# A perceiver block on one core: gates of the last three tiles ahead of tile 3, a semaphore for read banks, other banks for two tiles

## The reference

```
logits = x @ gate_w.T + gate_b                  # 8 per row
logits = where(in the top 2, logits, -inf)
gate   = softmax(logits)
out    = sum over e of gate[e] * (x @ expert_w[e] + expert_b[e])
x      = x + out
```

## Time and profile before

| | us |
|---|---|
| median of 3 runs | 988.33 |
| runs | 987.59 to 992.7 |
| the profiled execution | 989.81 |
| its span, first to last instruction | 988.1 |
| TensorE busy in the span | 920.4 (93%) |
| VectorE busy | 786.7 (80%) |
| ScalarE busy | 704.7 (71%) |
| GpSimd busy | 377.1 (38%) |
| mean granted TensorE clock | 0.977 |

### The profile page before, as it was taken

One profiled execution on the slowest core, in us unless ns is written; L12 is line 12 of the kernel. 1 busy time (PEld: TensorE's weight loads), 2 busy tenths in 40 slices (PEclk: granted clock), 3 DMA queues, 4 the chain that ended last, 5 costly groups with the idle time before them and its releaser, 6 DMA issues.

```text
span 988.1 us, 20490 instructions
## 1 busy us (share of the span) xinstructions
PE 920.4 (93%) x8246; PEld 494.5 (50%) x8246; DVE 786.7 (80%) x1591; ACT 704.7 (71%) x1003; POOL 377.1 (38%) x376
## 2 busy tenths in 40 slices
PE   7569999999999999999999999999999999979975
PEld 5344445454545454545454545454545454557742
DVE  5968898888787878797979797878786866668965
ACT  4566878787878787878787878787878667535631
POOL 6562034242524242424243425242424132253243
PEclk9799999999999999999999999999999999979987
DMA  6202031303030212120212121212122100000000
GB/s 206 68 17 64 4 88 12 80 12 81 12 79 16 77 17 75 18 74 19 74 19 74 20 72 19 74 24 68 24 56 29 29 1 23 1 23 23 2 6 16
DMA packets 74565, 41.95 MB, mean 42 GB/s; under 512 B 62276, under 2 KB 69864, under 8 KB 74472
## 3 DMA queue, kind: packets, MB, share of 16 engines
q1 hardware_dynamic: 74184, 39.60, 16.9%
q10 hardware_dynamic: 288, 1.05, 0.3%
HBM read 25.98 MB, written 0.59 MB: 27 GB/s over the span
## 4 chain that ended last, share of the span: by engine, by line
PE 66%; DVE 21%; ACT 5%; issue 4%; DMA 1%; POOL 1%; SPq 0%; POOLq 0%; ACTq 0%; DVEq 0%
PE S L2086 8%; PE S L2077 8%; PE S L2080 8%; PE OA L2110 7%; PE OA L2113 7%; PE OA L2116 7%; PE WW L2023 7%; DVE mx L1469 6%; DVE region L1481 4%; DVE region L1460 2%; ACT region L1791 2%; PE WW L2050 1%; PE WW L2051 1%; PE WW L2052 1%; DVE amx L764 1%
## 5 line engine op out<-in xcount | busy, mean ns | idle before, releaser
L1791 ACT ACTIVATE region<-S,sigma 128x1024 f16<-128x1024 f32 x208 | 231.9, 1115 | 155.5 <-PE S L2086 154.4
L1481 DVE TENSOR_TENSOR region<-S,region 128x1024 f16<-128x1024 f32 x208 | 252.5, 1214 | 72.6 <-ACT S L1795 72.6
L1469 DVE TENSOR_REDUCE mx<-WW 128x1 f32<-128x512 f32 (+1 forms) x480 | 259.8, 584 | 34.2 <-PE WW L2023 28.4
L1795 ACT ACTIVATE S<-S,sigma 128x1024 f32<-128x1024 f32 x208 | 225.3, 1083 | 0.0
L2077 PE MATMUL S<-region,xT 128*128 128x512 f16 (+1 forms) x416 | 124.2, 380 | 4.2 <-DVE region L1481 3.3
L2023 PE MATMUL WW<-xT,region 128*128 128x512 f16 x360 | 122.2, 381 | 4.1 <-DVE mx L1469 2.5
L2110 PE MATMUL OA<-region,xk 128*128 128x512 f16 (+1 forms) x416 | 124.2, 380 | 0.0
L2086 PE MATMUL S<-region,xT 128*128 128x512 f16 (+1 forms) x416 | 124.2, 380 | 0.0
L2113 PE MATMUL OA<-region,xk 128*128 128x512 f16 (+1 forms) x416 | 124.1, 380 | 0.0
L2116 PE MATMUL OA<-region,xk 128*128 128x512 f16 (+1 forms) x416 | 123.9, 379 | 0.0
L2080 PE MATMUL S<-region,xT 128*128 128x512 f16 (+1 forms) x416 | 123.7, 379 | 0.0
(11 more groups left out here) (315 smaller groups left out, 1800.6 us busy)
## 6 DMA issues: line engine op xcount, KB each, us to landing
raw<-ctx SPq DMA_DIRECT2D x16, 768.0 KB
rb<-inv_dram SPq DMA_DIRECT2D x16, 512.0 KB, 3.7
xT<-xk SPq DMA_TRANSPOSE x48, 3.3
left_row<-left_pT SPq DMA_DIRECT2D x48, 2.0 KB
raw<-ctx SPq DMA_DIRECT2D x16, 32.5 KB
WO_lo<-L_xattn_Wq ACTq DMA_DIRECT2D x1, 512.0 KB, 3.8
WO_hi<-L_xattn_Wkv ACTq DMA_DIRECT2D x1, 512.0 KB, 4.7
lx<-x SPq DMA_DIRECT2D x1, 512.0 KB, 8.3
```

Source lines behind the costliest of these rows:

```text
L1469: nc.vector.tensor_reduce(mx[:, r, c:c + 1], W[BANK[("m", n)]][:, 0:width], AX.X, ALU.max)\
L1481: nc.vector.tensor_tensor(p_lo[k], src, p_hi[k], ALU.subtract).then_inc(lo_done.sem, 1)
L1791: nc.scalar.activation(p_hi[k], src, ACT.Exp, scale=sigma[:, 0:1])
L1795: nc.scalar.activation(src, src, ACT.Exp, scale=sigma[:, 0:1]).then_inc(e_done.sem, 1)
```

## The change

- A semaphore `ex_read` is signalled by the eighth multiply-add of an odd tile, and VectorE waits on it instead of on its link. `experts(t)` of tiles 3 and 7 waits on `ex_read`; it no longer waits for the closing add.
- `weigh_experts` takes a first and a last expert, and the closing add is a function of its own, `close_experts`.
- VectorE: tile 1 is cut 4 + 2 + 2, with the last layer norm's normalisation behind the sixth; add_bias(0) and the closing of tile 1 come behind it. `side_reads(9)` and the gates of tiles 5 to 7 come ahead of all of tile 3, and add_bias(2) ahead of it as well.
- ScalarE: `exp(7, 1)` is moved behind `side_copies(6)`; `gate_columns(1)` ahead of `scale_experts(6)`.
- Banks: tile 5 takes the OA banks and tile 7 S banks 2 and 3; the gate columns of group 1 go to W[0] and their transposes wait for add_bias(2).
- TensorE: experts(2) ahead of the biases of tiles 0 and 1, experts(3) ahead of bias 2, experts(5) right behind experts(4), the gate transposes of group 1 ahead of experts(6), and the biases 4 and 5 ahead of experts(7).

```diff
@@ -546,6 +546,7 @@
         wt_t, wt_c = sem("wt_t"), sem("wt_c")
         lam_in, lam_exp = sem("lam_in"), sem("lam_exp")
         vb_clear = sem("vb_clear")
+        ex_read = sem("ex_read")
         LAST = Turn(B - 1)
         LAST_OUT = {("pj", 0): OA[:, 1, :]}
 
@@ -853,18 +854,22 @@
                     wait(dve, "gates", Turn(g))
                 return first_choice, second_choice
 
-            def weigh_experts(t, half):
-
-                if half == 0:
+            def weigh_experts(t, first, stop):
+                if first == 0:
                     dve.wait_ge(ex_mm.sem, t + 1)
-                for e in range(4 * half, 4 * half + 4):
+                for e in range(first, stop):
                     acc = xres[:, t, :] if e == 0 else xb[:, t, :]
                     ins = nc.vector.scalar_tensor_tensor(xb[:, t, :], expert_banks(t)[e // 4][:, D * (e % 4):D * (e % 4) + D],
                                                          lg[:, 7, t, e:e + 1], acc, ALU.mult, ALU.add)
-                    link(ins)
-                if half == 1:
-                    dve.wait_ge(ex_bias.sem, t + 1)
-                    nc.vector.tensor_tensor(xb[:, t, :], W[t % 2][:, 0:128], xb[:, t, :], ALU.add).then_inc(ex_odd.sem, 1)
+                    if e < NE - 1:
+                        link(ins)
+                    else:
+                        ins.then_inc(ex_read.sem, 1)
+                        dve.wait_ge(ex_read.sem, t // 2 + 1)
+
+            def close_experts(t):
+                dve.wait_ge(ex_bias.sem, t + 1)
+                nc.vector.tensor_tensor(xb[:, t, :], W[t % 2][:, 0:128], xb[:, t, :], ALU.add).then_inc(ex_odd.sem, 1)
 
             def add_bias(t):
                 dve.wait_ge(ex_bias.sem, t + 1)
@@ -901,23 +906,26 @@
             second0()
             group_norm(Turn(TB - 1))
             ln_normalise(dve, TB - 2).then_inc(ta["h2"].sem, 1)
-            weigh_experts(1, 0)
+            weigh_experts(1, 0, 4)
             side_reads(TB)
-            weigh_experts(1, 1)
+            weigh_experts(1, 4, 6)
             ln_normalise(dve, TB - 1).then_inc(ta["h2"].sem, 1)
+            weigh_experts(1, 6, NE)
             add_bias(0)
-            weigh_experts(3, 0)
+            close_experts(1)
             side_reads(SIDES)
             first1()
             second1()
-            weigh_experts(3, 1)
             add_bias(2)
-            weigh_experts(5, 0)
-            weigh_experts(5, 1)
+            weigh_experts(3, 0, NE)
+            close_experts(3)
+            weigh_experts(5, 0, NE)
             add_bias(4)
-            weigh_experts(7, 0)
+            close_experts(5)
+            weigh_experts(7, 0, 4)
             add_bias(6)
-            weigh_experts(7, 1)
+            weigh_experts(7, 4, NE)
+            close_experts(7)
 
 
         def tail_gpsimd(pool):
@@ -1020,6 +1028,8 @@
                 t = Turn(m)
                 if m > 1:
                     side_copies(m - 1)
+                if m == TB - 1:
+                    exp(t, 1)
                 if m - 1 == PJ_SIDE:
                     projected(LAST)
                 if m + 2 < TB:
@@ -1032,7 +1042,7 @@
                     exp(t.plus(1), 0)
                 weights(t, 2)
                 weights(t, 3)
-                if m + 1 < TB:
+                if m + 2 < TB:
                     exp(t.plus(1), 1)
                 if m == 1:
                     for k in range(2):
@@ -1048,8 +1058,8 @@
             gate_exponentials(1)
             scale_experts(4)
             wait(act, "gates", Turn(1))
+            gate_columns(1)
             scale_experts(6)
-            gate_columns(1)
 
 
         def project(t, dst):
@@ -1068,13 +1078,13 @@
             ins.then_inc(ta["projv"].sem, 1)
 
         def expert_banks(t):
-            if t == TB - 1:
+            if t == 5:
                 return [OA[:, k, :] for k in range(2)]
             return [S[:, 2 * (t % 2) + k, :] for k in range(2)]
 
         def gate_places(g):
 
-            return ((0, 0, 0, 4), (1, 128, 4, 1)) if g == 0 else ((1, 128, 5, 3),)
+            return ((0, 0, 0, 4), (1, 128, 4, 1)) if g == 0 else ((0, 128, 5, 3),)
 
         def tail_tensor(pe, side_item, weigh):
             mm = nc.tensor.matmul
@@ -1161,12 +1171,12 @@
                     pe.wait_ge(ld_ew.sem, 16)
                 if t < 2:
                     pe.wait_ge(ta["shifted"].sem, ta["shifted"].upto(Turn(TB - 1), t))
-                elif t == TB - 1:
+                elif t == 5:
                     wait(pe, "side1_out", side(SIDES))
                 elif t % 2 == 0:
                     pe.wait_ge(ex_scaled.sem, t // 2)
                 else:
-                    pe.wait_ge(ex_odd.sem, t // 2)
+                    pe.wait_ge(ex_read.sem, 1 if t == 3 else 2)
                 for c in range(2):
                     ins = mm(expert_banks(t)[c], hT[:, 128 * t:128 * t + 128],
                              ew[:, 4 * c:4 * c + 4, :].rearrange("p e o -> p (e o)"), start=True, stop=True)
@@ -1184,7 +1194,7 @@
                 if g == 0:
                     wait(pe, "t12", Turn(TB - 1))
                 if g == 1:
-                    pe.wait_ge(ex_odd.sem, 2)
+                    pe.wait_ge(ex_xb.sem, 2)
                 for bank, at, t, n in gate_places(g):
                     for k in range(n):
                         ins = nc.tensor.transpose(W[bank][0:NE, at + 128 * k:at + 128 * k + 128], lg[:, 7, t + k, :],
@@ -1233,24 +1243,25 @@
             side_transposes(TB)
             gate_transposes(0)
             side_products(TB)
+            experts(2)
             wait(pe, "gt", Turn(0))
             expert_bias(0)
             expert_bias(1)
-            experts(2)
             side_transposes(SIDES)
             side_products(SIDES)
+            experts(3)
             expert_bias(2)
-            experts(3)
             expert_bias(3)
             experts(4)
+            experts(5)
+            gate_transposes(1)
+            experts(6)
+            wait(pe, "gt", Turn(1))
             expert_bias(4)
-            experts(5)
-            experts(6)
+            expert_bias(5)
             experts(7)
-            gate_transposes(1)
-            wait(pe, "gt", Turn(1))
-            for t in range(5, TB):
-                expert_bias(t)
+            expert_bias(6)
+            expert_bias(7)
 
 
         block = es.enter_context(nc.Block())
```

## The result

The changed kernel takes 983.4 us (median of 8 runs, 977.72 to 986.37), the kernel before 990.72 in the same comparison; the ratio is 0.9935, interval 0.9918 to 0.9951. By the ratio, which leaves out one slow run of the kernel before (1202.84 us), it is 6.4 us faster. The forecast was 8.8 us, 979.5, and the range ended at 982.8.

A forecast was written before the change was run, and what follows sets the result against it. In the last 35 us TensorE and VectorE take turns, held by VectorE's queue order. Gains of 4.34, 4.6 and about 0.9 us, less 1.1 for the collision, make 8.8: from 988.33 to 979.5 us, range 976.3 to 982.8.

The forecast's parts named there:

- What bounds the kernel: Last 35 us: TensorE and VectorE take turns; VectorE stood 10.6 us for expert products, TensorE 5.16 us at expert_bias(4).
- the gates first: VectorE behind side 9: side_reads(9) starts 4.34 us earlier, then a plain sum of 14.33 us to the last add.
- TensorE's and the others' schedules: Behind side 9: TensorE at full clock supplies tiles 3 and 5 ahead, stalling VectorE 0.7 us at tile 7; ScalarE, GpSimd keep up.
- the tail: Start of side 6's transposes to the end of the span; forecast 8.8 us shorter.
- the tail of transfers: After the last two outputs are issued, the span ends 2.44 us later; claimed to stay.
- exp(7, 1) behind side_copies(6): ScalarE at side 6: copies begin about 0.65 us earlier, but side_reads(6) does not; gain 0, bounds -0.3 to +0.3 us.
- The collision: GpSimd's sum of tile 2 meets VectorE's gate operations in SBUF and slows them; 1.1 us, bounds 0 to 2.60.
- the upper bound of 2.6: Most the gates could lose to GpSimd's tile 2 sum: all of its 2.60 us.
- The rule of the Trainium skill: A VectorE operation with two SBUF inputs and a GpSimd operation reading SBUF exclude each other for the whole instruction.
- experts(2) ahead of the two biases: TensorE behind side 8: starts at 954.95 instead of waiting until 955.51 for gate columns; 0.56 us gained, counted as 0.5.
- rival 4: TensorE's clock stays at 0.50 from 953 to the end: median 989.1 us, slower; chance 0.02.
- The signs of being wrong: VectorE waiting over 1 us for an expert product behind the gates, or clock 0.50 between 961 and 972.

The follow-up runs named there:

- a_copy: The changed kernel run again unaltered, for a second profile; median 984.08 us, ratio 0.9949 to the kernel before.
- a_nocol: The changed kernel with GpSimd's sum of tile 2 held until the gates of tiles 5 to 7 are done; ratio 0.9935 to the kernel before.
- a_biasfirst: The changed kernel with experts(2) put back behind expert_bias(0) and (1); median 980.04 us, ratio 0.991 to the kernel before.
- a_copy2: The changed kernel run once more unaltered, in a later comparison; median 983.52 us, ratio 0.9918 to the kernel before.
- b_copy: The kernel before run again unaltered, for a second profile of it; ratio 0.9991.
- a_bf_nocol: The changed kernel with experts(2) back behind the first two biases and GpSimd's tile 2 sum held behind the gates; median 979.82 us, ratio 0.9895.
- b_gates: The kernel before with only VectorE's side_reads(9), gates of tiles 5 to 7 and add_bias(2) moved ahead of tile 3; ratio 0.9973.

## Why the prediction was wrong

*What bounds the kernel, the gates first, TensorE's and the others' schedules.* Right. In an execution whose clock returns as it did before, the tail is 8.9 us shorter against 8.8, VectorE waits for nothing behind the gates, and the last add ends 2.5 us before the end of the span (973.52), close to the 2.44 taken for the tail of transfers.

*exp(7, 1) behind side_copies(6).* Right: the products of side 6 start 1.18 us behind the transposes (935.98 - 934.80) instead of 1.79, and side_reads(6) 2.94 behind them (937.74) against 2.91. Gain 0. No run had it alone.

*The collision.* Right in place and size where the sum begins as forecast: 1.10 us. In a_copy it begins earlier in the gates and holds L839 (1.21 us), L844 (0.71) and L836 (0.29) instead. There the gates lose 1.7 us, less than the upper bound of 2.6. The rule of the Trainium skill named in the prediction (SBUF — State Buffer, section "SBUF: two separate sides") agrees, and a_nocol removes the collision by moving GpSimd alone.

*experts(2) ahead of the two biases.* This is the step that failed. I counted 0.5 us of gain, let the clock come back where it had, and reckoned everything behind at full clock. TensorE does resume 0.5 us earlier (17.0 us into the tail, where before had 955.51 - 937.99 = 17.5). But the return is then missed: 17.1 us at 0.50 instead of 6.8 in two of three profiles, and by the mean clock in 21 of 24 executions. Experts(3) and (4) are 1.7 us slower each, and VectorE, for which the sum had the products of tiles 3 and 5 ready 2 and 1 us ahead, waits 2.5 us in all, for tiles 5 and 7. The tail is 3.5 to 3.7 us longer (44.7 and 44.9 against 41.2). With the swap taken back (a_biasfirst) it is 41.4, so the edit that was to bring 0.5 costs about 3.

What happened is the mechanism of rival 4, the clock that stays at 0.50, cut short: the prediction adds there that with a return at 968 "the gain would still be some 5 us", and in a_copy the return comes 32.0 us into the tail, which is 970.0 in the times of before. I gave that rival 0.02, because in both cases seen the clock had risen "with TensorE working as densely as it would here". In a_copy TensorE works from 953.27 on with no wait but the 0.46 us ahead of 959.28, and the clock rises only at 968.3. The signs of being wrong that the prediction names are both there: a wait of 1.50 us for a product behind the gates, and a clock of 0.50 in the stretch that was to be at 1.00.

The size agrees roughly: of the forecast 8.8 us the usual execution loses 3.6, which leaves 5.2, and the three comparisons gave 6.4 (4.9 to 8.1), 5.0 (2.7 to 7.4) and 8.1 (5.5 to 10.7); the last begins just above it. Without the swap (a_biasfirst) the ratio gives 8.9 us. That its median, 980.0, lies so close to the forecast 979.5 is partly luck, as the forecast was counted from the low 988.33.

What stays open: why the clock returns in one execution of eight with the same program. It is not the waits, as the first profile and a_copy have the same ones in the same places (2.05 or 2.06, 0.86 or 0.87, and 0.46 us). What does differ in the rows is when the clock falls, counted from the end of that 2.05 us wait. In the four profiles of the changed kernel and a_nocol it is 0.7 us behind it in the first (the mean clock of 949 to 950 is 0.75), 1.0 in a_copy, 1.3 in a_nocol and 2.1 in a_copy2, and the last three missed the return. With the biases first the clock fell 0.7 to 1.3 us behind it in five profiles (before, b_copy, a_biasfirst, a_bf_nocol, b_gates) and came back after 6.8 us in each. No run set this moment, so that it decides is a guess.

## What to carry to other kernels

Where TensorE's clock drops, count the length of the slow stretch as a term of the sum with a range of its own, not as a constant: an edit worth half a microsecond inside it made it 10 us longer in most executions. The longest such stretch in both profiles of before (10.2 us, in the self attention) would still have been too short a bound for the 17.1 us here. Where work cannot be made dense, a dozen products nobody reads in the idle stretches kept the clock (5 to 6 us here). Before reading a profile as the kernel's behaviour, see by its time and its mean clock whether that execution is one of the usual ones.

## What was not expected of the hardware

The clock stayed at 0.50 for 17.1 us while TensorE's records fill 6.13 of 7, 2.54 of 3 and 8.00 of 8 us. It also dropped 0.7 us behind the end of a wait of only 2.05 us (the wait ends at 948.76 in the first profile; the mean clock of 946 to 950 is 0.94).

A VectorE operation of 24 elements, 0.18 us by itself, takes up to 1.21 us when it meets a sum of GpSimd's in SBUF (a_copy). L647, a normalisation of 128 elements a row in SBUF, takes 1.20 instead of 0.34 at 952.80 in the first profile, beside the sum of tile 0; VectorE had the time there, as it waited 1.76 us for the biases later. The multiply-adds of L862, which read PSUM and one SBUF operand, keep 0.34 to 0.35 us beside the same sums in all profiles.
